# An LSTM over 6,250 steps on one core: the cell's tanh taken by one activation a column, gates in the order i with f, g, o

## The reference, cut to what matters

```
x_proj = jnp.einsum('btd,gd->btg', x, W_ih) + b_ih + b_hh
def step(carry, xp):
    h, c = carry
    gates = xp + h @ W_hh.T
    i, f, g, o = jnp.split(gates, 4, axis=-1)
    c = jax.nn.sigmoid(f) * c + jax.nn.sigmoid(i) * jnp.tanh(g)
    h = jax.nn.sigmoid(o) * jnp.tanh(c)
    return ((h, c), h)
```

## Time and profile before

| | |
|---|---|
| median of 3 runs | 23927.46 us (23913.2 to 23932.15) |
| the profiled execution | 23903.88 us, its span 23901.7 us |
| LSTM, from the first to the last h | 10076.6 to 23736.2 us of the span |
| busy shares of the whole span | PE 79%, DVE 49%, ACT 38%, POOL 33% |

### The profile page before, as it was taken

How to read it: one execution, slowest core, us unless ns; L and a number is a source line. 1 busy time by engine, 2 the same in 40 slices (tenths; PEclk the granted TensorE clock), 3 DMA queues, 4 the chain that set the end, 5 groups by cost and what they waited for, 6 DMA issues and landing times. The chain is left out here.

```text
span 23901.7 us, 1177828 instructions
## 1 busy us (share of the span) xinstructions
PE 18780.0 (79%) x481492; PEld 14256.9 (60%) x481597; DVE 11724.7 (49%) x41911; ACT 8977.6 (38%) x40782; POOL 7768.2 (33%) x12838
## 2 busy tenths in 40 slices
PE   0000555668887777699999999999999999999998
PEld 0000333433334666377777777777777777777776
DVE  7500333357776555444444444444444444444445
ACT  0000000128884111144444444444444444444443
POOL 4776777317777777100000000000000000000000
PEclk9999777779999888799999999999999999999999
DMA  1000333200002333200000000000000000000000
GB/s 37 1 12 30 105 104 105 48 13 2 2 2 58 99 100 100 63 2 2 2 2 2 2 2 2 2 2 2 2 2 2 2 2 2 2 2 2 2 2 12
DMA packets 370442, 557.76 MB, mean 23 GB/s; under 512 B 177610, under 2 KB 254830, under 8 KB 369006
## 3 DMA queue, kind: packets, MB, share of 16 engines
q0 software_dynamic: 263728, 458.62, 7.7%
q1 hardware_dynamic: 106686, 98.81, 1.3%
HBM read 496.64 MB, written 60.32 MB: 23 GB/s over the span
## 5 line engine op out<-in xcount | busy, mean ns | idle before, releaser
L1196 PE MATMUL banks<-ls_xp,ls_sel 128*128 128x64 f32 x37500 | 5508.2, 283 | 69.5 <-DVE ls_w L1262 18.2
L1183 POOL TENSOR_TENSOR ls_d<-ls_tf,ls_cell 128x2 f32<-128x2 f32 x6250 | 1239.8, 198 | 12429.9 <-ACT ls_tf L1226 12429.9
L1196 PEld LDWEIGHTS banks<-ls_xp,ls_sel 128*128 128x128 f32 x37500 | 4654.0, 191 | 840.0 <-issue 183.8
L1211 PE MATMUL banks<-ls_w,ls_ht 128*2 128x64 f32 x200000 | 3930.7, 219 | 0.0
L471 PE MATMUL banks<-ag_rows,ag_pick 128*128 128x256 f32 x3328 | 1207.1, 526 | 3123.1 <-DMA ag_rows<-y_table,ag_idx 3093.9
L1268 DVE STREAM_TRANSPOSE ls_f_cols<-banks 128x64 f32<-128x64 f32 x6250 | 1558.9, 249 | 3331.6 <-PE banks L1205 3331.6
L1226 ACT ACTIVATE ls_tf<-ls_f_cols 128x2 f32<-128x2 f32 x6250 | 1283.7, 205 | 4917.0 <-DVE ls_f_cols L1268 4910.0
L1211 PEld LDWEIGHTS banks<-ls_w,ls_ht 128*2 128x2 f32 x200000 | 3093.1, 85 | 0.0
L471 PEld LDWEIGHTS banks<-ag_rows,ag_pick 128*128 128x128 f32 x3328 | 832.5, 262 | 3497.5 <-DMA ag_rows<-y_table,ag_idx 2490.2
L1205 PE MATMUL banks<-ls_w,ls_ht 128*1 128x64 f32 x100000 | 2519.9, 218 | 369.8 <-DVE ls_ht L1280 369.8
L1216 PE MATMUL banks<-ls_w,ls_ht 128*2 128x64 f32 x100000 | 2534.6, 219 | 0.0
(11 more groups left out here) (271 smaller groups left out, 21510.3 us busy)
## 6 DMA issues: line engine op xcount, KB each, us to landing
ag_rows<-y_table,ag_idx POOLq DMA_INDIRECT x1664, 2.7
mx_rows<-alpha_dst_table,mx_idx POOLq DMA_INDIRECT x1664, 2.3
at_rows<-wh_table,at_idx POOLq DMA_INDIRECT x1664, 2.8
projections<-xp_out SPq DMA_DIRECT2D x7, 3584.0 KB, 10.4
rec_table<-st_rec,st_idx POOLq DMA_INDIRECT x1563, 2.1
ls_xp<-projections SPq DMA_DIRECT2D x1250, 20.0 KB
rec_table<-zero POOLq DMA_DIRECT2D x5, 2496.0 KB, 17.7
rec_part<-rec_table SPq DMA_DIRECT2D x5, 2496.0 KB, 20.1
```

Of the source, the lines that this page charges most:

```text
L1196: x = nc.tensor.matmul(bank[:, 0:HD], sel[:, u, :], xp[:, b, lo:lo + HD], start=True, stop=False)
L1211: m = nc.tensor.matmul(banks_ig[s][32 * j:32 * j + 2, 0:HD], ht[:, v, c, 1 - r:3 - r], w[:, c, j, lo:lo + HD], start=False, stop=(r, c) == ...
```

## The change

In the LSTM the gates are regrouped: i and f share a bank (`banks_fi`), g has its own, o its own. PE computes i and f first, and waits for h column by column: the matmuls on column 0 may start as soon as that column is written. f and i are made by one Sigmoid activation (scale 2), g and o by Tanh as before. POOL writes f times c into `kept_part`. The scan is gone. The tanh of the new cell is one activation for each column, computing tanh(scale * in + bias) with in = tanh(g), scale = i and bias = kept_part, the last two read from SBUF as one number per partition. The cell itself is written by two more such activations with Identity. DVE makes h by one instruction for each column. The wake matmuls have 256 columns instead of 512, and 96 of them (24 times 4) are issued once ahead of the loop. One Sigmoid is run ahead of the loop too. In `stage_project` the loads of weights and biases are cut into four each, which puts the gates in the order i, g, f, o.

```diff
-            sp.dma_start(w[:, :, :], g["L1_ffn_W_ihT"].rearrange("(c p) n -> p c n", p=P)).then_inc(loaded, 16)
-            sp.dma_start(b_ih[:, :], g["L1_ffn_b_ihP"].to_broadcast([P, 4 * D])).then_inc(loaded, 16)
-            sp.dma_start(b_hh[:, :], g["L1_ffn_b_hhP"].to_broadcast([P, 4 * D])).then_inc(loaded, 16)
...
+            for tile, src in rows:
+                for to, of in ((0, 0), (HD, 2 * HD), (2 * HD, HD), (3 * HD, 3 * HD)):
+                    sp.dma_start(gates(tile)[:, :, to:to + HD], gates(src)[:, :, of:of + HD]).then_inc(loaded, 16)
...
@@ POOL
-                    pool.wait_ge(f_act, i * PER + (k + 1))
-                    nc.gpsimd.tensor_tensor(d1[:, 2:2 * SC:SC], tf[:, :], c_now, ALU.mult).then_inc(scan_in, 1)
+                    pool.wait_ge(cell_ready, i * (2 * PER) + (2 * k + 2))
+                    pool.wait_ge(fi_act, i * PER + (k + 1))
+                    nc.gpsimd.tensor_tensor(kept_part[:, :], fi[:, k % 2, 1, :], cell[:, :], ALU.mult).then_inc(cell_in, 1)
@@ PE
+            for n in range(WARM):
+                for j in range(4):
+                    nc.tensor.matmul(g["ps"][6][32 * j:32 * j + 1, 0:WAKE], wake[:, 0:1], wake[:, :], start=True, stop=True, tile_position=(0, 32 * j))
...
-                    pe.wait_ge(h_ready, i * PER + (k + 1))
-                    v = (k - 1) % (2 * LU)
+                    for c in range(2):
+                        pe.wait_ge(h_ready, i * (2 * PER) + (2 * k + c + 1))
+                        for r, lo in ((0, 0), (1, HD)):
+                            for j in range(4):
+                                m = nc.tensor.matmul(banks_fi[s][32 * j:32 * j + 2, 0:HD], ht[:, v, c, 1 - r:3 - r], w[:, c, j, lo:lo + HD],
+                                                     start=False, stop=(r, c) == (1, 1), tile_position=(0, 32 * j))
+                    m.then_inc(gates_ready, 1)
...
@@ ACT
+            nc.scalar.activation(tc[:, :], ht[:, 0, :, 1], ACT.Sigmoid)
...
-                    nc.scalar.activation(tf[:, :], tf_cols[:, 0:33:32], ACT.Tanh).then_inc(f_act, 1)
+                    nc.scalar.activation(fi[:, s, :, :], fi_cols[:, :].rearrange("p (c m) -> p m c", c=2)[:, 0:2, :], ACT.Sigmoid, scale=2.0).then_inc(fi_act, 1)
...
-                    act.wait_ge(scanned, i * PER + (k + 2))
-                    nc.scalar.activation(tc[:, :], c_now, ACT.Tanh).then_inc(tc_ready, 1)
-                    nc.scalar.copy(d1[:, 3:2 * SC:SC], c_now)
+                    act.wait_ge(cell_in, i * (2 * PER) + (2 * k + 2))
+                    for c in range(2):
+                        nc.scalar.activation(tc[:, c:c + 1], tg[:, s, c:c + 1], ACT.Tanh, bias=kept_part[:, c:c + 1], scale=fi[:, s, 0, c:c + 1]).then_inc(tc_ready, 1)
+                    for c in range(2):
+                        nc.scalar.activation(cell[:, c:c + 1], tg[:, s, c:c + 1], ACT.Identity, bias=kept_part[:, c:c + 1], scale=fi[:, s, 0, c:c + 1]).then_inc(cell_ready, 1)
@@ DVE
-                    dve.wait_ge(scan_in, i * (2 * PER) + (2 * k + 2))
-                    vec.tensor_tensor_scan(cell[:, :], d0, d1, 0.0, ALU.mult, ALU.add).then_inc(scanned, 1)
-                    dve.wait_ge(tc_ready, i * PER + (k + 1))
-                    vec.scalar_tensor_tensor(out=ht[:, k % (2 * LU), :, 1], in0=to[:, :], scalar=1.0, in1=tc[:, :],
-                                             op0=ALU.add, op1=ALU.mult).then_inc(h_ready, 1)
+                    for c in range(2):
+                        dve.wait_ge(tc_ready, i * (2 * PER) + (2 * k + c + 1))
+                        vec.scalar_tensor_tensor(out=ht[:, k % (2 * LU), c:c + 1, 1], in0=to[:, c:c + 1], scalar=1.0, in1=tc[:, c:c + 1],
+                                                 op0=ALU.add, op1=ALU.mult).then_inc(h_ready, 1)
```

More of the change, by code:

```diff
@@ L1063, in _, with gates @@
         def _(sp):
-            sp.dma_start(w[:, :, :], g["L1_ffn_W_ihT"].rearrange("(c p) n -> p c n", p=P)).then_inc(loaded, 16)
-            sp.dma_start(b_ih[:, :], g["L1_ffn_b_ihP"].to_broadcast([P, 4 * D])).then_inc(loaded, 16)
-            sp.dma_start(b_hh[:, :], g["L1_ffn_b_hhP"].to_broadcast([P, 4 * D])).then_inc(loaded, 16)
+            def gates(v):
+                return v.rearrange("p (j k) -> p j k", j=4)
+            rows = [(w[:, c, :], g["L1_ffn_W_ihT"][c * P:(c + 1) * P, :]) for c in range(2)]
+            rows += [(b_ih[:, :], g["L1_ffn_b_ihP"].to_broadcast([P, 4 * D])), (b_hh[:, :], g["L1_ffn_b_hhP"].to_broadcast([P, 4 * D]))]
+            for tile, src in rows:
+                for to, of in ((0, 0), (HD, 2 * HD), (2 * HD, HD), (3 * HD, 3 * HD)):
+                    sp.dma_start(gates(tile)[:, :, to:to + HD], gates(src)[:, :, of:of + HD]).then_inc(loaded, 16)
             with sp.Fori(0, NG) as i:
@@ L1097, in _ @@
             dve.wait_ge(evac, 4)
[L1098 removed]
+            dve.wait_ge(loaded, 16 * 16)
             vec.tensor_tensor(b_ih[:, :], b_ih[:, :], b_hh[:, :], ALU.add).then_inc(step, 1)
@@ L1102, in _ @@
             for row in (w[:, 0, :], w[:, 1, :], b_ih[:, :]):
-                for a, b in ((0, 2 * HD), (3 * HD, 4 * HD)):
+                for a, b in ((0, HD), (2 * HD, 4 * HD)):
                     v = row.rearrange("p (j k) -> p j k", j=4)[:, :, a:b]
@@ L1140, in stage_lstm @@
 def stage_lstm(nc, sb, sem, g):
-    R = 8
+    R, WAKE, WARM = 8, 256, 24
     w = sb("ls_w", [P, 2, 4, D])
@@ L1144, in stage_lstm @@
     sel = sb("ls_sel", [P, LU, P])
[L1145 to L1149, removed]
+    fi_cols, g_cols, o_cols = sb("ls_fi_cols", [P, HD]), sb("ls_g_cols", [P, HD]), sb("ls_o_cols", [P, HD])
+    fi, tg, to, tc = sb("ls_fi", [P, 2, 2, 2]), sb("ls_tg", [P, 2, 2]), sb("ls_to", [P, 2]), sb("ls_tc", [P, 2])
+    kept_part, cell = sb("ls_fc", [P, 2]), sb("ls_cell", [P, 2])
     ht = sb("ls_ht", [P, 2 * LU, 2, 3])
     free = sb("ls_free", [P, 1])
[L1152 to L1157, removed]
+    wake = sb("ls_wake", [P, WAKE], BF16)
+    banks_fi, banks_g, banks_o = [[g["ps"][3 * s + k] for s in range(2)] for k in range(3)]
+    w_loaded, zeroed, selected, xp_used, gates_ready, turned, fi_act, cell_in, cell_ready, tc_ready, h_ready, kept = (sem("ls_" + n) for n in (
+        "w_loaded", "zeroed", "selected", "xp_used", "gates_ready", "turned", "fi_act", "cell_in", "cell_ready", "tc_ready", "h_ready", "kept"))
     xp_in = [sem("ls_xp0"), sem("ls_xp1")]
@@ L1199, in _ @@
                     for j in range(4):
-                        nc.tensor.matmul(g["ps"][6][32 * j:32 * j + 1, :], wake[:, 0:1], wake[:, :], start=True, stop=True, tile_position=(0, 32 * j))
-                    pe.wait_ge(h_ready, i * PER + (k + 1))
-                    v = (k - 1) % (2 * LU)
+                        nc.tensor.matmul(g["ps"][6][32 * j:32 * j + 1, 0:WAKE], wake[:, 0:1], wake[:, :], start=True, stop=True, tile_position=(0, 32 * j))
+                    for c in range(2):
[5 more added lines that the diff above has]
+                    m.then_inc(gates_ready, 1)
                     for c in range(2):
                         for j in range(4):
-                            m = nc.tensor.matmul(banks_f[s][32 * j:32 * j + 1, 0:HD], ht[:, v, c, 1:2], w[:, c, j, HD:2 * HD],
+                            m = nc.tensor.matmul(banks_g[s][32 * j:32 * j + 1, 0:HD], ht[:, v, c, 1:2], w[:, c, j, 2 * HD:3 * HD],
                                                  start=False, stop=c == 1, tile_position=(0, 32 * j))
[L1207 to L1212, removed]
                     m.then_inc(gates_ready, 1)
@@ L1242, in _ @@
             vec.memset(xp[:, :, :], 0.0).then_inc(zeroed, 1)
[L1243 to L1246, removed]
+            vec.memset(sel[:, :, :], 0.0).then_inc(selected, 1)
+            dve.wait_ge(selected, 1)
             for j in range(4):
                 for r in range(2):
-                    m = vec.tensor_copy(sel[:, :, 32 * j + r], g["ident"][:, 2 * j + r:2 * j + r + R * (LU - 1) + 1:R])
-            m.then_inc(zeroed, 1)
-            vec.memset(ht[:, :, :, :], 0.0)
+                    vec.tensor_copy(sel[:, :, 32 * j + r], g["ident"][:, 2 * j + r:2 * j + r + R * (LU - 1) + 1:R]).then_inc(selected, 1)
+            vec.memset(cell[:, :], 0.0).then_inc(cell_ready, 2)
             vec.memset(wake[:, :], 1.0)
[L1253 to L1257, removed]
+            vec.memset(ht[:, :, :, :], 0.0).then_inc(h_ready, 2)
             dve.wait_ge(w_loaded, 16)
@@ L1262, in _ @@
                 vec.tensor_scalar(v, v, scale, None, ALU.mult).then_inc(zeroed, 1)
-            dve.wait_ge(zeroed, 5)
+            dve.wait_ge(zeroed, 4)
             with dve.Fori(0, N // PER) as i:
@@ L1267, in _ @@
                     dve.wait_ge(gates_ready, i * (3 * PER) + (3 * k + 1))
-                    vec.transpose(tf_cols[:, :], banks_f[s][:, 0:HD]).then_inc(turned, 1)
+                    vec.transpose(fi_cols[:, :], banks_fi[s][:, 0:HD]).then_inc(turned, 1)
                     if k % LU == 0:
```

25 lines of the change are left out of this document (13 added, 12 removed).

## The result

The changed kernel is slower: 24094.12 us, the median of 4 runs (24059.85 to 24102.96), against 23929.81 us before; the ratio is 1.0066 with a 95% interval of 1.005 to 1.0082. The forecast was 24200 us, 270 us above before; 164 us were measured, 0.7%.

What follows compares the result with a forecast made beforehand. The LSTM's ring from h to h was taken as the bound. Table load -456 us and longer ring about +718 gave +262, plus 15 done once: 24181 us, forecast as a median of 24200 us, range 23240 to 24450.

Steps and rivals of the forecast that it cites:

- the ring: LSTM step from one h to the next, through PE, transpose, tanh, scan, tanh of the cell and h: 2.11 us before.
- The price of two operands from SBUF: Scale and bias read by the tanh of the cell add up to 0.187 us, 0.093 each, in length and spacing.
- Rival (a): Tanh of the cell reads both operands together for 0.093 us: period 2.075 us, median 23270 us; chance 0.25.
- The period: LSTM loop, time of one step in the changed kernel: 2.225 us, against 2.11 before.
- the spacing of the two tanh activations: On ACT, the second column's tanh of the cell starts 0.11 + 0.187 us behind the first.
- the 0.03 us a turn that I kept for the branches: At the loop's turn, 0.03 of the missing 0.76 us stays because the loop's branches remain.
- what is done once: Outside the loop: warm-up matmuls delay the first step some 5 us, the cut loads in the projection stage 10 us.
- the halved wake matmuls: On PE in each step, half as long as their 0.39 us and started at 1.60: they cost nothing.
- my 0.73 us for moving the load alone: At the loop's turn, the table load leaving the loop saves 0.73 us a turn, 456 us over 625 turns.
- Rival (d): A table load stays in the loop or a second comes, each costing more than a step; chance 0.02.
- What releases the tanh of the cell: On ACT, the first tanh of the cell starts at 1.31 us behind o's tanh, with POOL's 1.27 just behind it.
- the loss of the clock: PE falls back to 1.2 GHz with halved wake matmuls: +0.45 us a step at most, some +2800 us; chance 0.04.

Runs made afterwards that it cites:

- e3: The changed kernel with neither scale nor bias from SBUF in the tanh of the cell; 0.9486 of the kernel before, 12366.3 us from first to last h.
- e2: The changed kernel whose tanh of the cell reads only its bias from SBUF, no scale; 0.9701 of the kernel before, 12899.8 us from first to last h.
- e1: The kernel before with one tanh ahead of the LSTM's loop, so the table load leaves the loop; ratio 0.9848, 13263.6 us from first to last h.
- e8: The kernel before with the table load ahead of the loop and wake matmuls of 256 instead of 512 columns; 23450.33 us against 23915.92, ratio 0.9806.
- e5: The changed kernel without the Sigmoid ahead of the loop, so a table load stands at the loop's head again; 1.0327 of the kernel before.
- e6: The changed kernel with the tanh of gate o taken once ahead of the loop instead of in each step; 1.0043 of the kernel before.
- e9: The kernel before with the table load ahead of the loop and no wake matmuls; ratio 1.2878, 20538.4 us from first to last h.
- e4: The changed kernel, but PE waits for both columns of h ahead of its first matmul on h; 1.0623 of the kernel before, 2.433 us a step.
- e7: The changed kernel without the 96 warm-up matmuls ahead of the loop; 1.0057 of the kernel before, 13813.1 us from first to last h.

## Why the prediction was right

**The bound and the ring.** As forecast: all but 5 of the 156 us lie between the first and the last h, and PE's share of busy time, 97% before and after, said nothing about it.

**The price of two operands from SBUF.** The sum hung on it, and the case taken, that they add up to 0.187 us, is the measured one (186, 279 and 371 ns in e3, e2 and the changed kernel). The DVE rows pointed the right way from another engine. The page "ScalarE: Activation LUTs" of the Trainium skill, section "What ACT_TABLE_LOAD costs", gives 93 ns for each pointer operand; the trace agrees, for two as well. Rival (a), that both are read together, is out.

**Where the sum was 100 us too high.** The period was forecast as 2.225 and is 2.210. The term that was mis-sized is the spacing of the two tanh activations, 0.297 in the prediction against 0.279: I had added the operands to a spacing of 0.11. That was the spacing of instructions 0.20 long; of two activations without operands, 0.186 long, it is 0.09 (e3), and the overlap of 0.093 stays the same with both operands (0.371 less 0.279). Over 6,250 steps 0.015 us are 94 us. Another 19 us are the 0.03 us a turn that I kept for the branches: in the changed kernel all ten steps take 2.21, so nothing is left of it. 262 - 94 - 19 = 149, and 151 were measured. For what is done once I had 15 us, and 5 were measured. With these 10 the terms make 123 us; the sum of 24181 us was 121 above the profiled execution.

**The turn.** I said of the halved wake matmuls that they cost nothing. In the old ring they also gain: with 512 columns 0.09 us of each turn stayed (2.20 against 2.11 in e1), and with 256 it is gone (e8). Beside the table load this did not count, so my 0.73 us for moving the load alone was too much: e1 gives 0.634, and with the wake matmuls halved as well, in e8, it is 458 us over 625 turns, 0.73. That the sum came out with 0.73 is thus luck, as the change halves the wake matmuls too. The changed kernel with 512 columns was not run. Rival (d) put a table load above a step; left in the loop it costs 1.04 us (e5), under half a step.

**What releases the tanh of the cell.** I named o's tanh, with POOL 0.04 us behind. Its start, 1.31 after the start of column 1's matmuls, was right, and the margin nearly: e6 has POOL 0.03 behind. What I had not foreseen in the expectation for e6 is that the activation itself gets 0.015 longer when it follows nothing at once, and that one step in ten hands over later.

**The clock.** It held, as forecast, but the ground was weak: I gave the loss of the clock 0.04 because PE idles little. e9 shows a PE that is busy all the time in the profile and stays at 1.2 GHz. My price for it, +0.45 us a step at most, left out the selecting matmuls, which in e9 cost 0.50 us of their own. The granted clock was 1.00 with wake matmuls of 512 columns (before) and of 256 (changed, e8), and 0.50 without any (e9); nothing between 256 and none was run.

**What is settled and what is not.** That the operands' price made the ring longer is shown by e2 and e3, and the 0.22 us of the early column by e4. The change was a gain of 458 us (load and wake matmuls, e8) and a loss of 609 us (13810.8 - 13201.2, the new ring against the old, both with the load and the smaller wake matmuls as in the change), where I had 456 and 718. What two instructions a column instead of one for both cost by themselves was not run, nor what POOL's part alone is worth. Why the step behind the first history copy starts 0.05 us later in e6, and not in the changed kernel, stays open.

## What to carry to other kernels

In a ring of tiny instructions the fixed time of each counts, and an operand read per partition is part of it: 93 ns each on ScalarE, in the length and in the spacing. Here the scan, 0.21 us ahead of the tanh, was folded into two activations with two such operands each. The ring grew by 0.10 us a step, although eight matmuls had left it. The same kernel with the old ring, the table load moved and the smaller wake matmuls (e8) is 1.9% faster than before. Look for what a loop's head repeats (here a table load in each of 625 turns) before rebuilding its body, and when a stall goes, look for the next one under it.

## What the runs showed of the hardware that was not expected

TensorE stayed at 1.2 GHz for 20.5 ms, from the first to the last h, while the profile had it busy 11000 of 11000 us in the stretch read (e9). It did the matmuls on h, whose stationary operand has one or two columns, and six records with 128 a step. With four bf16 matmuls of 256 columns a step more, the granted clock was 0.50 at the start and 1.00 some 10 us later (e7), and 1.00 in the stage (changed kernel, e8). A step took 2.11 us with them and 3.29 without (e8, e9).

An activation of one element with both operands took 371 ns right behind another instruction of ACT and 387 ns where it had to wait (e6).
